# Issuing the load of x's second half slice behind the first warm-up matmul, and one warm-up matmul fewer

## The reference, cut to what matters

```
base   = x @ W.T                       # 512 -> 512
logits = x @ Wr.T + 5 * onehot(ids)    # 8 experts
gates  = softmax over the top two of logits
h      = x @ A.T                       # 8 experts x 16
y      = base + 2 * (h * gates) @ B    # then a 4-bit quantized FFN 512 -> 1376 -> 512
x      = x + ffn0(y)
x      = x + ffn1(x @ w1[adapter].T)   # second layer, RMSNorm, 512 -> 1792 -> 512
```

## Time and profile before

| what | before |
|---|---|
| median of 3 runs | 444.74 us (444.53 to 444.99) |
| the profiled execution | 445.29 us |
| its span, first to last instruction | 443.5 us |
| outside the span | 1.8 us |
| PE busy, share of the span | 99% |
| DVE, ACT, POOL busy | 78%, 49%, 43% |
| granted TensorE clock | 1.000 |

### The profile page before, as it was taken

How to read it: one execution, slowest core, us unless ns; L and a number is a source line. 1 busy time by engine, 2 the same in 40 slices (tenths; PEclk the granted TensorE clock), 3 DMA queues, 4 the chain that set the end, 5 groups by cost and what they waited for, 6 DMA issues and landing times.

```text
span 443.5 us, 5522 instructions
## 1 busy us (share of the span) xinstructions
PE 439.6 (99%) x1954; PEld 358.9 (81%) x1954; DVE 345.6 (78%) x446; ACT 218.2 (49%) x285; POOL 192.8 (43%) x162
## 2 busy tenths in 40 slices
PE   8999999999999999999999999999999999999997
PEld 4688888888888888888888888888888888888886
DVE  3778999898876988949787668768688578999922
ACT  4514575665542212528577656456466554474200
POOL 0356888987007200900005869897997400000000
PEclk9999999999999999999999999999999999999999
DMA  8955112210007686287369617937568146885623
GB/s 272 227 165 175 52 49 80 86 48 0 2 1 254 205 314 256 82 303 304 119 238 327 241 47 225 338 125 267 182 210 273 60 144 262 342 292 182 217 105 142
DMA packets 30456, 79.98 MB, mean 180 GB/s; under 512 B 2384, under 2 KB 15840, under 8 KB 28768
## 3 DMA queue, kind: packets, MB, share of 16 engines
q1 hardware_dynamic: 26752, 68.24, 44.4%
q0 software_dynamic: 3104, 10.73, 8.0%
q10 hardware_dynamic: 576, 0.72, 0.5%
HBM read 58.95 MB, written 20.72 MB: 180 GB/s over the span
## 4 chain that ended last, share of the span: by engine, by line
PE 99%; DVE 0%; issue 0%; DVEq 0%
PE ps L1670 10%; PE ps L1930 10%; PE ps L1932 10%; PE ps L1931 10%; PE ps L1671 10%; PE ps L1674 10%; PE ps L2045 5%; PE ps L2044 5%; PE ps L1790 5%; PE ps L1792 5%; PE ps L1791 5%; PE ps L2043 5%; PE ps L1913 2%; PE ps L1911 2%; PE ps L1912 2%; PE ps L1681 1%
## 5 line engine op out<-in xcount | busy, mean ns | idle before, releaser
L1670 PE MATMUL ps<-h_hi,ring_hi 128*128 128x512 f32 x152 | 59.4, 391 | 0.0
L1671 PE MATMUL ps<-h_lo,ring_hi 128*128 128x512 f32 x152 | 59.2, 389 | 0.0
L1110 DVE TENSOR_TENSOR ring_lo<-raw,ring_hi 128x1792 fp32r<-128x1792 f32 (+3 forms) x24 | 47.1, 1966 | 11.1 <-ACT ring_hi L746 11.0
L1930 PE MATMUL ps<-zt_hi,ring_hi 128*128 128x512 f32 x140 | 54.6, 390 | 0.0
L1932 PE MATMUL ps<-zt_hi,ring_lo 128*128 128x512 f32 x140 | 54.5, 389 | 0.0
L1931 PE MATMUL ps<-zt_lo,ring_hi 128*128 128x512 f32 x140 | 54.5, 389 | 0.0
L746 ACT ACTIVATE ring_hi<-raw 128x1792 fp32r<-128x1792 f32 (+1 forms) x23 | 36.6, 1593 | 23.5 <-PE ps L1932 10.1
L1674 PE MATMUL ps<-h_hi,ring_lo 128*128 128x512 f32 x152 | 47.8, 389 | 0.0
L636 POOL DMA_INDIRECT scale<-in_sc_gu,idx_gu x20 | 27.6, 1380 | 23.6 <-DVE idx_dn L1147 16.6
L1670 PEld LDWEIGHTS ps<-h_hi,ring_hi 128*128 128x128 f32 x152 | 28.5, 188 | 6.7 <-issue 0.5
L1674 PEld LDWEIGHTS ps<-h_hi,ring_lo 128*128 128x128 f32 x152 | 28.5, 188 | 6.0
(11 more groups left out here) (252 smaller groups left out, 1111.1 us busy)
## 6 DMA issues: line engine op xcount, KB each, us to landing
ad_raw<-in_w1T SPq DMA_DIRECT2D x8, 1024.0 KB, 5.9
wd<-down_weights SPq DMA_DIRECT2D x7, 1024.0 KB, 5.6
down_weights<-dhi SPq DMA_DIRECT2D x7, 896.0 KB, 4.6
down_weights<-dlo SPq DMA_DIRECT2D x7, 896.0 KB, 4.0
raw<-in_gu SPq DMA_DIRECT2D x12, 512.0 KB, 3.6
wd<-down_weights SPq DMA_DIRECT2D x7, 768.0 KB, 5.6
draw<-in_d SPq DMA_DIRECT2D x7, 512.0 KB, 4.3
dn_work<-in_qw_dn SPq DMA_DIRECT2D x11, 256.0 KB
```

Of the source, the lines that this page charges most:

```text
L1110: dve.tensor_tensor(dst, src, hi_part.bitcast(F32), ALU.subtract).then_inc(done_sem, 1)
L1670: pe.matmul(ps[:, bank + hf, :], w_hi, v_hi[:, t], start=first, stop=False)
L1671: pe.matmul(ps[:, bank + hf, :], w_hi, v_lo[:, t], start=False, stop=False)
L1930: pe.matmul(ps[:, bank, :], ring1_hi[s][:, w], z_hi[:, t], start=first and k == 0, stop=False, skip_group_check=True)
```

## The change

SP waits for the first tick, that is the end of the first warm-up matmul, between the loads of x0 and x1, so that x1 and all of SP's later issues stand behind that wait. PE makes seven warm-up matmuls with a tick instead of eight; the one that waits for x0 stays.

```diff
             load_x(0)
+            sp.wait_ge(s_tick, 1)
             load_x(1)
             sp.dma_start(aw_raw[:, aw_cols(1)], a["aw"][:, aw_cols(1)]).then_inc(s_aw[1], 16)
             for i in range(2, len(X_PIECES)):
...
             pe.wait_ge(s_warm, 1)
-            for _ in range(8):
+            for _ in range(7):
                 pe.matmul(ps[:, 0, :], warm[:, 0:P], warm, start=True, stop=True).then_inc(s_tick, 1)
             pe.wait_ge(s_x[0], 16)
             pe.matmul(ps[:, 0, :], warm[:, 0:P], warm, start=True, stop=True)
```

## The result

The changed kernel takes 446.40 us (median of 7 runs, 445.69 to 446.61), against 444.74 for the kernel before (7 runs, 444.34 to 445.02). The ratio is 1.0036, with a 95% interval from 1.0025 to 1.0047: 1.7 us slower, clear of the 0.2% that can be told from no change. The forecast was 444.8, range 444.2 to 445.6. The time lies outside it.

The account below looks back on a forecast made before the run. TensorE, busy 99% of the span, bounds the kernel. Main line 0 to 0.1 (x2 +0.2 less slack 0.1 to 0.2) and zero points 0 gave +0.05 on 445.29, which lies 0.55 over the median: 444.8, range 444.2 to 445.6.

Parts of the forecast that it names:

- What bounds the kernel: Whole span: TensorE, busy 99%, makes up the chain that ended last; only its waits in the first stages can move.
- the four named: TensorE's early waits: x0's landing, the first product at 5.24, slice 1's weight load at 10.99, the first FFN matmul at 44.42.
- (c): Slice 1's weight load at 10.99: idle 0.41 for x's high part, behind ScalarE's 1.68 wait for x2 until 9.56.
- The tick and SP's delay: SP's queue at the start: tick at 1.84, x1's issue 0.66 later at 1.85, all behind it up to 0.66 later.
- x0's gain: First load: lands 0.1 earlier without x1 beside it, bounds 0 and 0.47; worth nothing unless x2 lands earlier.
- So no gap opens and the same bytes end at the same time: DMA engines, early loads: x0 and aw(0) last to about 3.4, x1's data come at 2.9; lower bound of x2's shift 0.
- the 0.2 for x2 in the sum: TensorE's main line: x2 lands 0.2 later; less slack of 0.1 to 0.2 this leaves 0 to 0.1.
- The upper bound of 0.66 for x2's landing: x2's load: at most the whole 0.66 shift, if the delay of issue passed through.
- The change of order: x2 and ScalarE's aw(2) change places in the queues: x2 at 9.8 at the latest, 0.24 later, taken as 0.2.
- The zero points: Second chain, to the first FFN matmul: their write, landing at 26.58, shifts by 0, bounds -0.3 and +0.66.
- The rival with the clock: TensorE before slice 1: a 0.4 gap before x0 lets the clock rise later; +1.5, 446.2, up to +3.4; chance 0.07.
- The rival "delay passes through": SP's loads: x2 and the zero points land 0.66 later; +0.6, 445.4; chance 0.13.

Follow-up runs that it names:

- The wait before x2: Against the kernel before: SP waits for tick 3 behind the loads of x1 and aw1, ahead of x2; 445.07 us, ratio 1.0014.
- the load of aw1 ahead of the wait: Against the changed kernel: SP issues aw1's load behind x0, ahead of its wait, with x1 still held; 444.48 us, ratio 1.0001.
- ScalarE's loads out of the way: Two kernels, against the changed kernel: ScalarE's aw2, aw3 and cst issued behind later ticks; 452.37 us, and 448.24 us in the milder form.
- the hold on one queue: Against the kernel before: SP waits behind x0 with eight warm-ups, and SP instead of ScalarE issues aw2, aw3 and cst; 445.48 us, ratio 1.0013.
- the kernel before once more: The kernel before, unchanged, run again for the spread of its own landings; 444.74 us, ratio 1.0004.
- seven with an idle wait: Against the changed kernel: SP waits for the cleared warm tile (1.15) instead of tick 1, seven ticking warm-ups; 444.63 us, ratio 1.0004.
- a longer one: Against the changed kernel: SP's wait at tick 2 (2.27) instead of tick 1 (1.85); 445.50 us, ratio 1.0016.

## Why the prediction was wrong

- **What bounds the kernel: right.** Time is only lost or won in TensorE's waits of the first stages: behind the first FFN matmul both kernels take the same 399 us. Of the four named, (c), the wait for x2, is where all of it came from: 1.37 at slice 1, 1.25 of it left at the first FFN matmul, 1.1 in the two spans (the kernel before was profiled in a late execution; the medians differ by 1.66).
- **The tick and SP's delay: right.** x1's issue ended at 2.18 and aw1's began at 2.23, so x1 was issued at some 1.8. x2's issue moved by 0.55, a little less than the 0.66 forecast, and so came level with aw(2)'s at 2.70 and not behind it.
- **x0's gain: not refuted, and not shown.** 0.18 where 0.1 was taken, between bounds 0 and 0.47, but against the second execution of the kernel before it is 0.05 later. The five rows with x1 held (four at tick 1, one at tick 2) had x0 at 4.31 to 4.59, the seven others at 4.44 to 5.04; the two overlap. That it is worth nothing by itself: right.
- **"So no gap opens and the same bytes end at the same time": wrong, and this is the step that failed.** The sign that the prediction had set for a delay, x2 landing after 10.1, came in at 10.94. It was argued from a mean rate: 464 KB of x0 and aw(0) at 290 GB/s would last to 3.4, and x1's data would come at 2.9. A hole opened all the same, from 4 to 5.5 us: 205 GB/s instead of 294. The argument took it that the engines run at the mean rate as long as some load is outstanding. Here x1, aw(1), x2 and aw(2) had all been issued by 3.2, and the engines still stood idle for 29% of that time. The wait before x2 and the load of aw1 ahead of the wait show that x1 may be late, or x2 may be late, as long as another load stands queued behind x0. So the term that failed is the 0.2 for x2 in the sum: it measured 1.38.
- **The upper bound of 0.66 for x2's landing: wrong.** A delay of issue was taken to pass through one for one at worst. It passed through at 2.5 for one (1.38 for 0.55): SP's queue was 0.35 MB short at 10 us and then moved 0.27 MB per us.
- **The change of order: the mechanism exists, but only beside the hole.** With SP's queue full, aw2 issued early leaves x2 at 9.10. With the hold, ScalarE's loads out of the way bring x2 from 10.94 to 9.81 or 10.37. Priced at 0.2, measured at 0.6 to 1.1 (0.9 against the hold on one queue), in kernels that differ in other things too.
- **The zero points: right by luck.** 26.43 against 26.58, but the kernel before once more had 23.45, so the agreement says nothing of the shift. In the other kernels this start moved between 23.05 and 27.87. Where it was late the chain did bind a little: with aw1 ahead of the wait, at 26.27, TensorE stood idle for 0.27 at the first FFN matmul and began it at 44.31, while the kernel before once more, 0.23 later at slice 1, began it at 43.99. That the chain has no slack was true of one execution and not of the kernel.
- **The rival with the clock: its price of +1.5 came near the measured +1.7, its mechanism is not the cause.** Seven matmuls alone 445.03 (ratio 1.0014), seven with an idle wait 444.63 (1.0004); the wait with eight matmuls has the whole loss. And the sign set for it, triples of half 0 over 1.2 us behind 7 us, is not there: from 7.32 on they take 0.84 to 0.86 in the changed kernel. The measured time happened to lie where the wrong rival pointed.
- **The rival "delay passes through": the right place with the wrong size.** It was given +0.6.

Of the Trainium skill's two rules, that of "DMA: Bandwidth & Descriptors", section "Queues, rings and completion order", on the order in a ring agrees with x0's start here: 4.49 with x1 held, 4.44 and 4.67 with x1 behind it. That of "TensorE: Matmul & The Clock Gate", Part 1, that time under load counts and not the number of matmuls, agrees with the first triples of all kernels that ran: 0.92 to 1.65 us with seven warm-up matmuls, 0.93 to 1.62 with eight.

**What stays open.** That too little queued behind x0 makes the hole is shown, by adding a load there and by moving the wait. Why the hole reaches from 4 to 5.5 us, 2 us after x1's issue and with four loads outstanding, is not; nor why the rate from 6 to 10 us is 300 to 350 after one hold and 400 after a longer one. And the depth of the hole doesn't order the losses: 151 GB/s on one queue went with a ratio of 1.0013, 205 in the changed kernel with 1.0036.

## What to carry to other kernels

At the head of a kernel, holding a load back to let the first one land sooner bought at most a few tenths here and can open a hole in the transfers that is filled late or not at all. Look at the wait that ends last in the stage: if it is for a later load, idle time of the DMA engines before that load counts, here more than once over, and the first load's gain counts for nothing. If a load must be held, put another that is needed anyway ahead of the wait. And bound a delayed issue by what the engines can move meanwhile, and not by the delay.

## What the runs showed of the hardware that I had not expected

- A DMA engine share of 0.53 to 0.74 from 4 to 5.5 us, with loads issued from 1.84 to 2.70 still outstanding. With x1 issued at about 2.27, it served ScalarE only at 7.96.
- The same pair of ScalarE's DMA issues took 0.85 us at 2.70 and 2.40 us at 4.41, and blocked the engine that issued them.
- The rise of TensorE's clock from 1.2 to 2.4 GHz differs between executions with the same warm-up: the first three products took 0.94 in the kernel with the wait before x2 (three at the higher level take 0.84 later on), 1.28 and 1.51 in two executions of the kernel before, and 1.62 in the changed kernel, with the granted clock at 1.00 in each. Seven or eight warm-up matmuls had both kinds.
